# Loading the second expert behind the last row stores, and three expert matrices in sixteen pieces each

## The chip, the cores and the metric

The kernel runs on one core of a Trainium2 chip. The metric is the device time of one execution in microseconds (us). Before the change the median of three runs is 1216.72 us (1214.84 to 1219.3).

## What is computed

The input `x` is 2 sequences of 2048 tokens with 512 features (4096 tokens in all). One decoder layer in three stages, each fed by a layer norm and added back to `x`:

```
x = x + attn(layernorm(x))          # gated linear recurrence along the sequence
x = x + xattn(layernorm(x), ctx)    # 16 heads, 77 context tokens, causal mask
x = x + ffn(layernorm(x))           # mixture of 4 experts, the best 2 for each token

def ffn(x):                         # xf: the 4096 token rows
    gate_scores = xf @ gate_W + gate_b
    topk_scores, topk_idx = top_k(gate_scores, 2);  weights = softmax(topk_scores)
    h   = relu(layernorm(xf @ W1[e] + b1[e]) * g1[e] + be1[e])
    y_e = layernorm(h @ W2[e] + b2[e]) * g2[e] + be2[e]
    return xf + sum over the 2 chosen experts of weight * y_e
```

Each expert has two 512 x 512 matrices, W1 and W2. Everything is float32; the kernel splits each operand into a high and a low part and sums three products of the parts.

## The kernel before, in words

**Stages.** Stage A (the recurrence) and stage B (attention) each go over the tokens in 8 chunks of 512 (`NCH = 8`, `TPC = 4` tiles of 128 tokens in each). During stage A the eight expert matrices are split into high and low parts and stored in DRAM as `expert_parts` (`ws_d`), 2 MB for each matrix. Stage C is the mixture: 67 expert tiles (`NSLOT`), each with 128 rows of one expert. In stage B each token is given places in a slot table in DRAM, through indirect DMAs of GpSimd (`scatter`, L2513). The tokens of the first four chunks fill "early" tiles 0 to 28 (`EARLY = 29`), which are worked off from expert 0 to expert 3; the other 38 tiles follow, again from expert 0 to 3.

**One expert tile i** (`c_tile`): SyncE loads its 1 KB of slot entries (`load_slots`, L606); VectorE copies them to an index for the gather five tiles ahead (`gather_rows`, called in `c_tile` i - 5); GpSimd gathers the 128 rows (L2557, 256 KB); TensorE transposes them (`rows_in`, L1109), makes the first product with W1 (`first_product`, two tiles ahead, 12 matmuls at L1097), the transposes of the hidden rows (`hidden_in`, L1125) and the second product with W2 (`second_product`, 12 matmuls at L1097). So on TensorE the matmuls of `first_product(i + 2)` and `second_product(i)` stand together, 24 in one group. VectorE and ScalarE norm and scale. GpSimd adds the result rows to the output in DRAM with an indirect DMA that accumulates (`add_out`, L2576), and before it issues one it waits until the one before has landed: `need(pool, added[1 - u], 16 * (n + u))`. Behind that wait on GpSimd's own queue stand the next tile's reciprocal root (`rstd`, L2585), its gather and its slot scatter.

**Who waits for the weights.** The matrices have numbers s = 0 to 7: s = 2e is W1 of expert e and s = 2e + 1 its W2. SyncE raises `experts_ready` by one for each, in this order (`expert_in`). `first_product` waits for `experts_ready >= 2e + 1` (L1113) and `second_product` for `>= 2e + 2` (L1130). All DMAs that SyncE issues go to one queue, in program order, and a wait on SyncE holds everything written behind it.

**SyncE around the change.** It works off one written list (L613 to L669): matrix 0, the bias rows b1, slot pairs 0 to 2, matrix 4, row stores of chunk 6 (`store_xf` L547 to `xf_rows`, `store_base` L554 to the output), b2, matrix 1, more row stores, slot pairs 3 and 4, matrix 3, the last row stores, a wait for the base rows (`base_out`, L643), the g2 rows, and then matrices 2, 5, 6 and 7 between slot pairs 5 to 13. A slot pair is the loads of tiles 2n and 2n + 1, and a slot load waits for the one two before it. Behind the last matrix stand the four base stores of chunk 7, the waits for all row stores and for the slot table, and then the slot loads of tiles 28 to 66, of which tile 28's is first wanted in `c_tile` 23. ScalarE loads the be2 rows on its own queue (L1531) once the last `xf_rows` stores have landed.

Of the kernel before, what the change touches and what calls it, by code (L numbers as in the profile page):

```python
# [17 lines left out]
F32, F32R, I32 = mybir.dt.float32, mybir.dt.float32r, mybir.dt.int32  # L18
# [4 lines left out]
P = 128  # L23
B, S, D = 2, 2048, 512
T = B * S
KC = D // P
# [23 lines left out]
EARLY = 2 * EARLY_CH * TPC - (NE - 1)  # L50
# [16 lines left out]
def need(engine, semaphore, value):  # L67

    if isinstance(value, int) and value <= 0:
        return  # L70
    engine.wait_ge(semaphore, value)
# [9 lines left out]
def decoder_layer(nc, io, out, scratch_kind="Internal"):  # L81
    ctx = ExitStack()
    with ctx:
# [3 lines left out]
        def sem(name):  # L87
            return ctx.enter_context(nc.semaphore(name))
# [4 lines left out]
        def dram(name, shape, dt):  # L93
            return nc.dram_tensor(name, shape, dt, kind=scratch_kind).ap()
# [6 lines left out]
        ws_d = dram("expert_parts", [2 * NE, 2, KC, P, D], F32)  # L101
# [10 lines left out]
        def r_at(kb, n):  # L112
            return R[:, int(kb * KB_):int(kb * KB_) + n]
# [52 lines left out]
        weights = r_at(8, 4 * NE * KC * D).rearrange("p (w e a k f) -> p w e a k f", e=NE, w=2, a=2, k=KC)  # L166
# [122 lines left out]
        w_in = [sem(f"w_in{i}") for i in range(2 * NE)]  # L289
# [45 lines left out]
        def in_front(order, c):  # L335

            if isinstance(c, int):
                return sum(len(groups_of(order, i)) for i in range(-1, c))
            return in_front(order, 2) + (c - 2) * len(order)

        def index_in(order, c, name):
            return [g for g, _ in groups_of(order, c)].index(name)
# [5 lines left out]
        def mm_num(c, name):  # L348

            return in_front(MM_ORDER, c) + index_in(MM_ORDER, c, name)  # L350
# [4 lines left out]
        def last_in_bank(order, c, name):  # L355

            before_c = c - 1 if isinstance(c, int) else 1 if len(groups_of(order, 1)) == len(order) else 2
            own = groups_of(order, c)
            at = index_in(order, c, name)
            older = [] if isinstance(c, int) and c < 0 else groups_of(order, before_c)  # L360
            row = older + own[:at]
            same = [i for i, (_, bank) in enumerate(row) if bank == own[at][1]]
            return in_front(order, c) - len(older) + same[-1] + 1 if same else 0
# [7 lines left out]
        def slot3(c):  # L371

            return ring[:, (c + NCH) % 3] if isinstance(c, int) else ring[:, bass.ds((c + NCH) % 3, 1)].rearrange(
                "p r j f -> p (r j) f")
# [50 lines left out]
        def _(sp):  # L425
# [19 lines left out]
            for hl in range(HPG):  # L445
                rows = slice(hl * DH, (hl + 1) * DH)
# [103 lines left out]
            def store_base(c, j, rows=None):  # L550

                t = 4 * c + j
                need(sp, base_ready, t + 1)
                sp.dma_start(out_v[t] if isinstance(t, int) else out_v[bass.ds(t, 1)].rearrange("n p f -> p (n f)"),  # L554
                             base[:, j % 2] if rows is None else rows).then_inc(base_out[j % 2], 16)
# [31 lines left out]
            def load_expert(s):  # L587

                e, w = s // 2, s % 2
                sp.dma_start(weights[:, w, e].rearrange("p a k f -> p (a k) f").bitcast(F32),  # L590
                             ws_d[s].rearrange("a k p f -> p (a k) f")).then_inc(w_in[s], 16)

            def expert_in(s):
                sp.wait_ge(w_in[s], 16)
                sp.sem_inc(experts_ready, 1)

            def load_rows(dst, name, loaded):
                sp.dma_start(dst, io[name].rearrange("e f -> (e f)").partition_broadcast(P).rearrange(
                    "p (e f) -> p e f", e=NE)).then_inc(loaded, 16)

            def load_slots(n, u):

                i = 2 * n + u
                row = sp.value_load(plan_row[0:1, bass.ds(i, 1)], min_val=0, max_val=NE * REG - P)
                need(sp, slots_in[u], 16 * n)
                sp.dma_start(tile_slots[:, bass.ds(i, 1), :].rearrange("p i w -> p (i w)"),  # L606
                             slots_d[bass.ds(row, P), :]).then_inc(slots_in[u], 16)

            def load_slot_pairs(first, end):
                for n in range(first, end):  # L610
                    for u in range(2):
                        load_slots(n, u)
# [7 lines left out]
            sp.wait_ge(plan_ready, 1)  # L620
            load_slot_pairs(0, 3)
            expert_in(0)
            sp.wait_ge(s_done, 2 * KC * NCH)
            load_expert(4)
# [8 lines left out]
            for j in range(2):  # L633
                store_base(last - 1, j, slot3(last - 1)[:, j, :])
            load_slot_pairs(3, 5)
            load_expert(3)
            for j in range(2, TPC):
                store_base(last - 1, j, slot3(last - 1)[:, j, :])
            sp.wait_ge(mm_done, mm_num(NCH, "o3") + 1)
            for j in range(TPC):  # L640
                store_xf(last, j)
            for i in range(2):
                sp.wait_ge(base_out[i], 16 * 2 * last)  # L643
            load_rows(g2_rows, "L0_ffn_g2", g2_in)
            expert_in(1)
            load_slot_pairs(5, 7)
            load_expert(2)
            load_slot_pairs(7, 9)
            for s in range(2, 5):
                expert_in(s)  # L650
            for s in range(5, 2 * NE):
                load_expert(s)
                load_slot_pairs(2 * s - 1, min(2 * s + 1, EARLY // 2))
                expert_in(s)
            for j in range(TPC):
                store_base(last, j, slot3(last)[:, j, :])
# [1981 lines left out]
```

## Time and profile before

| | us |
|---|---|
| median of 3 runs (range) | 1216.72 (1214.84 to 1219.3) |
| the profiled execution's own time | 1209.59 |
| its span | 1207.8 |
| TensorE (PE) busy | 1159.6 (96%) |
| VectorE (DVE) busy | 924.9 (77%) |
| ScalarE (ACT) busy | 731.5 (61%) |
| GpSimd (POOL) busy | 457.2 (38%) |

How to read it: the span is the stretch of the profiled execution from its first to its last instruction, and every time in rows counts in us from its start. PE is busy nearly all the time, so what can be saved are its few idle stretches; an idle stretch of another engine costs nothing by itself. PEclk is the clock that TensorE was granted, 1.00 being 2.4 GHz and 0.50 being 1.2 GHz. "To landing" is the time from the issue of a DMA to its arrival.

### The profile page before, as it was taken

How to read it: one execution, taken by the hardware profiler on the slowest of the kernel's cores; microseconds unless marked ns; L12 is line 12 of the kernel's file. 1: busy time of each engine (PE TensorE's matmuls, PEld its weight loads, DVE VectorE, ACT ScalarE, POOL GpSimd, SP SyncE). 2: the span in 40 equal slices, each digit the busy share in tenths (PEclk: the TensorE clock that was granted, in tenths of full speed). 3: DMA queues.
4: the chain of work that ended last, by engine and by line, in shares of the span. 5: the costliest groups of instructions: out<-in, count | busy, mean ns of one | idle time of the engine just before them, and what ended most of it. 6: DMA issues, size and time to landing. Idle time of an engine off the chain costs nothing.

```text
span 1207.8 us, 24523 instructions
## 1 busy us (share of the span) xinstructions
PE 1159.6 (96%) x6041; PEld 978.9 (81%) x6042; DVE 924.9 (77%) x2196; ACT 731.5 (61%) x2114; POOL 457.2 (38%) x410
## 2 busy tenths in 40 slices
PE   6999999999989999999999998989999999999993
PEld 5788888888878888888888877867888888888882
DVE  6888888887766677877868777678777777777774
ACT  5323333233486757767677662567777777777773
POOL 4040000000052314535445164357655555555543
PEclk9999999999999999999999998899999999999998
DMA  8754544444520302133021358885554444444433
GB/s 271 230 160 160 188 176 146 174 156 165 199 84 1 105 10 97 44 107 104 10 97 44 131 131 227 270 221 122 81 88 81 85 79 86 80 85 80 85 64 42
DMA packets 83237, 143.90 MB, mean 119 GB/s; under 512 B 20460, under 2 KB 24752, under 8 KB 82309
## 3 DMA queue, kind: packets, MB, share of 16 engines
q1 hardware_dynamic: 63872, 101.60, 25.8%
q0 software_dynamic: 18464, 39.14, 17.1%
q10 hardware_dynamic: 837, 2.41, 0.6%
q8 instruction: 28, 0.46, 0.2%
q14 instruction: 36, 0.29, 0.1%
HBM read 78.83 MB, written 67.83 MB: 121 GB/s over the span
## 4 chain that ended last, share of the span: by engine, by line
PE 83%; DMA 5%; DVE 4%; issue 3%; ACT 3%; POOL 2%; POOLq 0%; DVEq 0%; SPq 0%; ACTq 0%
PE banks L1097 27%; PE banks L681 21%; PE banks L746 7%; PE banks L891 6%; PE banks L879 5%; DMA out<-rows,scatter_rows 4%; PE banks L848 3%; PE banks L865 3%; PE banks L1109 2%; PE banks L907 2%; PE banks L1125 2%; ACT rows L1310 2%; PE banks L719 1%; PE banks L800 1%; PE banks L765 1%
## 5 line engine op out<-in xcount | busy, mean ns | idle before, releaser
L1097 PE MATMUL banks<-operands 128*128 x1608 | 388.6, 396 | 10.5 <-DVE operands L1570 5.2
L1097 PEld LDWEIGHTS banks<-operands 128*128 128x128 f32 x1608 | 298.1, 189 | 73.6 <-issue 7.4
L681 PE MATMUL banks<-operands 128*128 128x512 f32 (+2 forms) x1224 | 292.6, 394 | 3.5 <-DVE operands L1570 3.5
L681 PEld LDWEIGHTS banks<-operands 128*128 128x128 f32 (+1 forms) x1224 | 225.6, 192 | 47.8 <-DVE operands L1570 3.7
L1570 DVE TENSOR_TENSOR operands<-banks,operands 128x512 fp32r<-128x512 f32 (+3 forms) x328 | 217.7, 682 | 42.5 <-ACT operands L1189 38.8
L1189 ACT ACTIVATE operands<-banks 128x512 fp32r<-128x512 f32 (+3 forms) x328 | 191.7, 608 | 96.7 <-PE banks L879 45.0
L1310 ACT ACTIVATE rows<-banks,score_shift 128x77 f32<-128x77 f32 x512 | 162.7, 374 | 28.0 <-DVE score_shift L1792 27.2
L1189 ACT ACTIVATE operands<-rows 128x512 fp32r<-128x512 f32 (+3 forms) x79 | 55.3, 709 | 163.8 <-DVE rows L1641 138.1
L1495 ACT ACTIVATE banks<-banks,param_cols 128x128 f32<-128x128 f32 x268 | 99.2, 430 | 82.5 <-PE banks L1125 82.5
L2576 POOL DMA_INDIRECT out<-rows,scatter_rows x67 | 106.6, 1591 | 104.2 <-DVE rows L2315 65.1
L1310 ACT ACTIVATION_READ_ACCUMULATOR rows<-banks,score_shift 128x1 f32 x512 | 129.1, 256 | 0.0
L2500 POOL TENSOR_TENSOR rows<-rows,score_rec 128x1232 f32<-128x1232 f32 x32 | 72.1, 2253 | 147.3 <-DVE score_rec L1800 147.3
L2262 DVE BATCH_NORM_STATS2 moe_stats<-banks 128x6 f32<-128x512 f32 x134 | 93.2, 695 | 43.9 <-PE banks L1097 42.5
L891 PE MATMUL banks<-operands 128*128 128x512 f32 x384 | 97.7, 406 | 0.0
L746 PE MATMUL banks<-operands 128*128 128x512 f32 x384 | 91.6, 394 | 0.1
L2585 POOL TENSOR_TENSOR moe_rstd<-moe_var_eps,minus_half 128x2 f32<-128x2 f32 (+1 forms) x70 | 52.4, 748 | 83.8 <-DVE moe_var_eps L2275 83.8
L746 PEld LDWEIGHTS banks<-operands 128*128 128x128 f32 x384 | 70.9, 188 | 15.7 <-DVE operands L1570 1.3
L891 PEld LDWEIGHTS banks<-operands 128*128 128x128 f32 x384 | 72.0, 194 | 14.2
L2557 POOL DMA_INDIRECT rows<-xf_rows,gather_rows x67 | 69.3, 1034 | 30.8 <-issue 24.9
L879 PE MATMUL banks<-operands 103*128 103x512 f32 (+1 forms) x288 | 75.6, 403 | 2.0 <-DVE operands L1783 1.4
L2460 POOL TENSOR_TENSOR ln_rstd<-ln_var_eps,minus_half 128x4 f32 (+1 forms) x8 | 10.1, 1262 | 170.8 <-DVE ln_var_eps L1665 170.8
L2513 POOL DMA_INDIRECT slot_table<-slot_payload,slot_rows x64 | 65.1, 1018 | 19.8 <-issue 13.7
(178 smaller groups left out, 1707.0 us busy)
## 6 DMA issues: line engine op xcount, KB each, us to landing
expert_parts<-operands SPq DMA_DIRECT2D x32, 512.0 KB, 3.0
operands<-expert_parts SPq DMA_DIRECT2D x8, 2048.0 KB, 11.1
rows<-in_x SPq DMA_DIRECT2D x8, 1024.0 KB, 5.4
rows<-in_L_ffn_W SPq DMA_DIRECT2D x32, 256.0 KB, 3.5
x_rows<-rows SPq DMA_DIRECT2D x8, 1024.0 KB, 4.3
rows<-x_rows SPq DMA_DIRECT2D x8, 1024.0 KB, 5.7
xf_rows<-rows SPq DMA_DIRECT2D x32, 256.0 KB, 2.7
out<-rows SPq DMA_DIRECT2D x32, 256.0 KB, 2.5
```

Of the source, the lines that this page charges most:

```text
L681: last = nc.tensor.matmul(dst, stationary(a, k), moving(b, k), start=(t == 0 and k == 0), stop=(t == len(terms) - 1 and k == n_k - 1))
L746: last = nc.tensor.matmul(g_bank[m % 2], wg[:, a, k, m * P:(m + 1) * P], hTr[:, a2, k, :], start=(k == 0 and t == 0), stop=(k == KC - 1 an ...
L879: last = nc.tensor.matmul(mb(c, f"v{m}"), vblk[0:n, a, m, u, :], pT[0:n, a2, u, :], start=(t == 0 and u == 0), stop=(t == len(TERMS) - 1 a ...
L891: last = nc.tensor.matmul(mb(at, f"o{j}"), out_part(c, a, m)[:, j * P:(j + 1) * P], wo[:, a2, m, :], start=(m == 0 and t == 0), stop=(m == ...
L1097: last = nc.tensor.matmul(dst, stationary[:, a, k, :], weights[:, w, bass.ds(e, 1), a2, k, :].rearrange("p e f -> p (e f)"), start=False, ...
L1189: return nc.scalar.activation(dst, src, ACT.Copy, scale=scale)
L1310: nc.scalar.activation(pb[m % 2][:, j, keys], s_banks[:, j, keys], ACT.Exp, bias=nmax[:, m % 2, at], scale=-1.0, accum_out=ssum[:, m % 2, ...
L1495: nc.scalar.activation(ch_bank[:, at], ch_bank[:, at], ACT.Relu, scale=pcol[:, bass.ds(e * KC + (ROW_G1 + k), 1)], bias=pcol[:, bass.ds(e ...
L1570: return V.tensor_tensor(dst, src, hi.bitcast(F32), ALU.subtract)
L2262: V.bn_stats(c_st[:, which, :], src).then_inc(stat, 1)
L2500: G.tensor_tensor(p3, p3, srec[:, m % 2, :].unsqueeze(2).to_broadcast([P, TPC * HPG, SK]), ALU.mult).then_inc(p_ready, 1)
L2576: G.indirect_dma_start(out, bass.IndirectOffsetOnAxis(six[u][:, 0:1], 0), y2[u], None, compute_op=ALU.add).then_inc(added[u], 16)
```

## The change

Four things are changed, all in SyncE's list.

- Matrix 3 (W2 of expert 1) is no longer loaded between slot pair 4 and the last base stores of chunk 6, but behind the g2 rows and matrix 2.
- `expert_in(1)` moves ahead of the wait for the last projection and the row stores of chunk 7.
- Slot pairs 5 to 8 come in one row behind matrices 2 and 3, where matrix 2 stood between pairs 6 and 7.
- Matrices 5, 6 and 7 are not one DMA of 2 MB each, but sixteen of 64 partitions x 2 KB (128 KB) each. Before each piece but the first SyncE waits until the piece before has landed, so one is in flight at a time. A slot pair follows each half of a matrix, and `expert_in(s)` waits for all sixteen.

```diff
+            PIECES = 4 * KC
+
+            def load_expert_parts(s, parts):
+                e, w = s // 2, s % 2
+                for n in parts:
+                    a, k, rows = n // (2 * KC), n // 2 % KC, slice(n % 2 * (P // 2), (n % 2 + 1) * (P // 2))
+                    need(sp, w_in[s], 16 * n)
+                    sp.dma_start(weights[rows, w, e, a, k, :].bitcast(F32), ws_d[s, a, k, rows]).then_inc(w_in[s], 16)
+
             def expert_in(s):
-                sp.wait_ge(w_in[s], 16)
+                sp.wait_ge(w_in[s], 16 if s < 5 else 16 * PIECES)
                 sp.sem_inc(experts_ready, 1)
...
             load_slot_pairs(3, 5)
-            load_expert(3)
             for j in range(2, TPC):
                 store_base(last - 1, j, slot3(last - 1)[:, j, :])
+            expert_in(1)
             sp.wait_ge(mm_done, mm_num(NCH, "o3") + 1)
             for j in range(TPC):
                 store_xf(last, j)
             for i in range(2):
                 sp.wait_ge(base_out[i], 16 * 2 * last)
             load_rows(g2_rows, "L0_ffn_g2", g2_in)
-            expert_in(1)
-            load_slot_pairs(5, 7)
             load_expert(2)
-            load_slot_pairs(7, 9)
+            load_expert(3)
+            load_slot_pairs(5, 9)
             for s in range(2, 5):
                 expert_in(s)
             for s in range(5, 2 * NE):
-                load_expert(s)
-                load_slot_pairs(2 * s - 1, min(2 * s + 1, EARLY // 2))
+                for half_n in range(2):
+                    pair = 2 * s - 1 + half_n
+                    load_expert_parts(s, range(PIECES // 2 * half_n, PIECES // 2 * (half_n + 1)))
+                    load_slot_pairs(pair, min(pair + 1, EARLY // 2))
                 expert_in(s)
```

## Rows read from the trace of the kernel before

**Rows 1.** The page, busy time of each engine (share of the span), instructions.
```profile
PE 1159.6 (96%) x6041; PEld 978.9 (81%) x6042; DVE 924.9 (77%) x2196; ACT 731.5 (61%) x2114; POOL 457.2 (38%) x410
```

**Rows 2.** TensorE's timeline, 736 to 880: start, us, line, operation, [idle before <-releaser].
```profile
753.53 0.66 PE L1109 MATMUL banks<-ident,rows 128*128 128x128 f32 x4 [2.39 <-DMA rows<-xf_rows,gather_rows]
...
759.27 7.40 PE L1097 MATMUL banks<-operands 128*128 x24
...
768.53 5.78 PE L1097 MATMUL banks<-operands 128*128 x24
...
788.18 1.20 PE L1097 MATMUL banks<-operands 128*128 x4 [1.98 <-DVE operands L1570]
...
803.51 1.79 PE L1097 MATMUL banks<-operands 128*128 x4 [2.29 <-DVE operands L1570]
...
819.04 1.19 PE L1097 MATMUL banks<-operands 128*128 x4 [0.92 <-DVE operands L1570]
...
827.50 5.71 PE L1097 MATMUL banks<-operands 128*128 x24
...
833.84 5.73 PE L1097 MATMUL banks<-operands 128*128 x24
```

**Rows 3.** The chain that ended last, 690 to 1210: start, us, what.
```profile
784.25 4.92 DMA out<-rows,scatter_rows
790.02 8.94 DMA out<-rows,scatter_rows
...
903.95 5.46 PE banks L1097 x24
```

**Rows 4.** GpSimd's timeline, same columns as TensorE's.
```profile
743.30 0.98 POOL L2557 DMA_INDIRECT rows<-xf_rows,gather_rows  x1 [0.30 <-issue]
```

**Rows 5.** Waits, 700 to 1210: us in total, times, longest.
```profile
POOL out L2576 <- DMA out<-rows,scatter_rows: 21.5, 11, 4.3
```

**Rows 6.** Windows of 4 us: PE, PEld, DVE, ACT, POOL, PEclk, DMA share, GB/s.
```profile
756.00:760.00 4.00, 4.00 (x19) 3.90 (x20) 1.05 (x4) 0.21 (x1) 2.00 (x2) 0.51 1.03 412
760.00:764.00 4.00, 4.00 (x13) 3.14 (x12) 1.98 (x11) 0.56 (x1) 0.00 (x0) 0.64 1.00 319
```

**Rows 7.** SyncE's timeline, 650 to 1210: first start, us to the last issue's end.
```profile
742.44 0.43 SPq L590 DMA_DIRECT2D operands<-expert_parts  x1
...
744.08 3.85 SPq L547 DMA_DIRECT2D xf_rows<-rows  x4
756.23 0.34 SPq L598 DMA_DIRECT2D rows<-in_L_ffn_g  x1
...
775.65 0.40 SPq L590 DMA_DIRECT2D operands<-expert_parts  x1
...
802.41 0.40 SPq L590 DMA_DIRECT2D operands<-expert_parts  x1
...
815.19 1.90 SPq L554 DMA_DIRECT2D out<-rows  x4
872.55 63.17 SPq L606 DMA_DIRECT2D rows<-slot_table  x39
```

**Rows 8.** SyncE's waits, 650 to 1000: us in total, times, longest.
```profile
SPq L643 <- DMA out<-rows: 8.2, 1, 8.2
```

**Rows 9.** DMA issues, 742 to 744.3: count, KB each, median us to landing.
```profile
operands<-expert_parts SPq DMA_DIRECT2D x1, 2048.0 KB, 12.4
```

**Rows 10.** DMA issues, 802 to 803, and then 815 to 818.
```profile
operands<-expert_parts SPq DMA_DIRECT2D x1, 2048.0 KB, 12.7
...
out<-rows SPq DMA_DIRECT2D x4, 256.0 KB, 2.6
```

**Rows 11.** The page, DMA issues of the whole span: two loads of 1 MB and 256 KB.
```profile
rows<-in_x SPq DMA_DIRECT2D x8, 1024.0 KB, 5.4
...
rows<-in_L_xattn_Wq SPq DMA_DIRECT2D x4, 256.0 KB, 2.7
```

**Rows 12.** Line L466, eight single loads of 256 KB into SBUF.
```profile
DMA to landing us min/median/max: 2.5/2.7/4.3
```

## Prediction

> **What bounds the kernel now.** I read the page first: TensorE is busy for 1159.6 of 1207.8 us [rows 1], so only its idle stretches (and its slow ones) can be won. Next I read TensorE's timeline where the expert matrices are loaded. The reader is to see there that a tile in the undisturbed stretch takes 833.84 - 827.50 = 6.34 us, while from 768.53 to 827.50 eight tiles take 58.97 us instead of 8 x 6.36 = 50.9 (6.36 is the mean of twelve tiles, (903.95 - 827.50) / 12 = 6.37) [rows 2, 3]. That is 8.1 us lost, with idle stretches of 1.98, 2.29 and 0.92 us in the middle of the second product. The trace names VectorE for them; the chain of waits and GpSimd's waits say who is behind it: the accumulating DMA takes 8.94 us instead of 4.92 when it meets a matrix of 2 MB (one row stands for three alike), and GpSimd waits 21.5 us for it in all [rows 3, 5]. The next tile's reciprocal root stands behind that wait, and the hidden rows behind the root. Ahead of this a gather issued at 743.30 lands only when TensorE has waited 2.39 us for it, at 753.5: matrix 3 was issued just before it, at 742.44 [rows 2, 4, 7]. Last I read SyncE's timeline, for when each matrix is issued, and the DMA issues for how long each size takes.
>
> **Part 1: matrix 3 moves behind the row stores.** The gather of 743.30 then meets only six row stores of 256 KB, and at less than half its present 10 us it is there before TensorE asks at 751.1: -2.4 us. The stretch is also the one after which the granted clock fell to 0.51 and 0.64 [rows 6], and the 24 matmuls of 759.27 took 7.40 instead of 5.7 us [rows 2]. If less idle time keeps the clock up, about 1.7 us more is won here; I leave that out of the sum, since other idle time stays in the stretch, and keep it for the lower end.
>
> SyncE gains too. It waited 8.2 us for base stores that were queued with matrix 3 [rows 8], so the g2 rows go out at about 748.0 (744.08 + 3.85) instead of 756.23, and matrices 2 and 3 by 748.9 [rows 7]. The queue then holds 1 + 2 + 2 MB, and the be2 rows (1 MB) come on ScalarE's queue. Matrix 3 took 12.4 us with 1.5 MB of stores about it, so 3.5 MB in 12.4 us [rows 9]; 5 MB take 18 us by this, 6 MB 21. I take 19: all in at 767.5. Eight slot loads stand behind; the first two are issued at once, the third waits for the first, which lands behind the matrices. The other six cost 1.62 us each (39 of them in 63.17 us [rows 7]), less a little: SyncE reaches the pieces at T0 = 776 us, 770 to 781. It was 775.65 when matrix 5 went out before [rows 7], so SyncE arrives at the same time with matrix 3 behind it. `expert_in(2)` comes at T0 as well. It is wanted by `first_product(5)` in `c_tile` 3, which began two tiles behind 768.53 (`c_tile` 1 [rows 2]), at 781.3, and after part 1 begins at about 779: hidden, with 3 us to spare. It costs what T0 is later than that, up to 2 us. `expert_in(1)` moves past nothing that anybody waits for: matrix 1 is long in, and TensorE did not wait for it. The larger risk of the part is that the next gathers now meet 5 MB. The program issues a gather two tiles, 12.7 us, ahead of its use, and that of 743.30 took 10 us in like company [rows 2, 4], so nothing.
>
> **Part 2: what the pieces remove.** Between 776 and 815 three loads of 2 MB filled the queue. In pieces of 128 KB, one in flight, an accumulating DMA meets at most one piece on each engine. I take 4.9 to 5.5 us for it, against the 6.36 of a tile: GpSimd no longer falls behind and the 8.1 us go. The bounds of this term are 0 (pieces disturb as much as whole matrices) and -8.1. Together G = 2.4 + 8.1 = 10.5 us.
>
> **Part 3: what the pieces add.** SyncE now pays one full flight for each of 48 pieces where it paid three such as 12.7 us [rows 10]. The trace shows no 128 KB load, so it is bounded. Single loads of 256 KB landed in 2.5 us at least, 2.7 in the median, 4.3 at worst [rows 12]. From 1 MB at 5.4 to 256 KB at 2.7 is 2.7 us for 768 KB, so half of 256 KB saves 0.45 us [rows 11]: 2.05 to 2.25 us. Beside the mixture's gathers and accumulating DMAs four stores of 256 KB landed in 2.6 at 815 us [rows 10], which is no more than the loads' median, so for that company I add only 0.1 to the upper of the two. To this comes 0.08 us from landing to the next issue (the last matrix: 802.41 + 12.7 = 815.11, next issue 815.19 [rows 7, 10]). One step is then t = 2.4 us. Its bounds are 2.1, and 2.9 if the pieces meet the other DMAs at every step. A slot pair takes 2 x 1.62 + 0.4 us of SyncE beside one flight, so each of the five pairs adds 3.6 - t = 1.2.
>
> All of matrix 7 is in at A = T0 + 48 t + 5 (3.6 - t) = 776 + 115.2 + 6 = 897 us, where it was 815.1.
>
> **When is it wanted?** From the reference's inputs the two choices of the first 2048 tokens are 697, 1052, 1151 and 1196 for experts 0 to 3, in whole tiles 5, 8, 8 and 9. So expert 1 starts at tile 5, expert 2 at 13, expert 3 at 21. Tile 9's group began at 827.50 and tile 21's at 903.95 [rows 2, 3]; the second product is its later half, so in the old time W2 of expert 3 (matrix 7) is wanted at 906.8. Matrix 6 is wanted in `c_tile` 19, at 891; matrix 5 in `c_tile` 13, at 856. They arrive at T0 + 32 t + 5 = 858 and 817: both hidden. The slots of tile 26, wanted in `c_tile` 21, go out at T0 + 40 t + 6 = 878: hidden until t is over 2.7.
>
> With a gain G ahead of tile 21 everything is wanted G earlier, and matrix 7 holds TensorE if it is later. The two do not add up; the change in the end is the larger of -G and A - 906.8. That is the larger of -10.5 and -9.8: **about 1 us of stall, net -9.8**. For one more microsecond or so of stall and clock I take -8.5. Slot loads of tiles 28 and on come behind A, four stores (1.90 us) and their landing (2.6), at about 903, where they began at 872.55 [rows 7, 10]. Tile 28's is wanted in `c_tile` 23, old time 916.6, new 906.6, and needs some 3 us more: hidden by about 1 us, and if matrix 7 is late, that moves with it.
>
> **A rule of the skill.** The Trainium skill, "DMA: Bandwidth & Descriptors", section "Rules for kernel authors", speaks against the change: merge small transfers, at least 1 MiB for full bandwidth. The trace agrees as to bandwidth (2 MB in 12.4 to 12.7 us [rows 9, 10] against 16 x 2.4 = 38). Its section "Anatomy of one DMA" gives about 2.0 us and bytes / 436 GB/s for the GpSimd path; that would be 2.3 us for a piece, an estimate by that page, and with the 0.08 A = 896, the same case.
>
> **Rivals.**
> 1. *The weights' own latency takes the gain.* At t = 2.6, A = 906.7: the end does not move at all, and from there each 0.1 us in t costs 4.3 us. In t = 2.48 to 2.7 the result is within 6 us of before, -6 to +5. For it: 256 KB loads were 2.7 in the median. Against it: half the bytes.
> 2. *Slower.* The one mechanism is the same wait, of `second_product(21)` for `experts_ready >= 8`, at t over 2.73 (or 2.6 with T0 six us late). At t = 2.9, A = 776 + 139.2 + 3.5 = 918.7: +12 us, and after such an idle stretch the clock may fall as in [rows 6], +2: **+14**. For it: 256 KB took 4.3 us at worst [rows 12]. Against it: the median of eight is 2.7.
> 3. *The pieces disturb as much as the matrices did*, and the change doesn't do what it says. Then G = 2.4 and the end moves by -2.4, no more, as matrix 7 is wanted at 904. Against it: at most a few packets lie ahead of an accumulating DMA.
> 4. *All hidden, and the clock stays up*: G = 12.2 and t of 2.3 or less, -12.
>
> **How the numbers follow.** Forecast (with rival 4): 50%. Rival 1: 18%. Rival 3: 8%. Rival 2: 24%, as one number multiplied by 48 decides, and T0 shifts it too. The sum is made against the profiled execution: span 1207.8, own time 1209.6, so it would come out at 1201.1. The median of the runs shown is 1216.7, 7.1 above that execution, and the same change on it gives **1208.2 us**. The low end is rival 4's -12: 1204.5. The high end reaches into rival 2, +12: 1228.5. The likeliest case alone is 1204.5 to 1211. 0.5% is 6.1 us, about what a measurement of this kernel can tell from no change: faster 0.50, same 0.25, slower 0.25.
>
> **What would show it.** Right: the waits for L2576 by GpSimd shrink from 21.5 us to under 8; no accumulating DMA of 8.9 us; the gather of tile 3 in under 6 us and no 2.39 on L1109; SyncE's pieces from about 776, 2.4 us apart; TensorE's only wait for experts is at tile 21 and is under 3 us. Wrong: pieces over 2.6 us apart, with a hole in TensorE before the second product of tile 21, of the size A - 896; a hole before tile 5's first product (T0 late); or idle time on L1097 as before with no long transfer on SyncE's queue.

## The result, and the profile after

The changed kernel takes 1254.89 us in the median of 4 runs (1251.24 to 1256.15), beside 1217.97 us for the kernel before on the same chip (the three runs shown ahead and one more). The ratio is 1.0302 with a 95% interval of 1.0271 to 1.0333: 37 us slower, where I had forecast 8.5 faster. The measured time also lies above the range (1204.5 to 1228.5).

The page of the profile after. Its span is 46.0 us longer than before, at the same work of TensorE (1163.3 us where [rows 1] have 1159.6). Five loads of 2 MB are left of the eight.

```profile
span 1253.8 us, 24568 instructions
PE 1163.3 (93%) x6041; PEld 979.5 (78%) x6042; DVE 925.7 (74%) x2196; ACT 731.0 (58%) x2114; POOL 455.3 (36%) x410
...
operands<-expert_parts SPq DMA_DIRECT2D x5, 2048.0 KB, 9.2
```

The waits after, 700 to 1250 us (us in total, times, longest). TensorE waits for SyncE three times, 45.6 us in all, which is about the size of the difference. (Added up: its busy time grew by 3.7 us and its idle time by 42.3, of which the 45.6 are one part and 3.3 us less of other idle time the other.) VectorE's waits for slot entries (22.3 us) fall in the same stretch; none of them shows in TensorE's waits. GpSimd's wait for its accumulating DMAs, the thing the pieces were to cure, is down from 21.5 us [rows 5] to 15.0.

```profile
PE banks L1108 <- SPq L605: 45.6, 3, 27.1
...
DVE gather_rows L2292 <- DMA rows<-slot_table: 22.3, 3, 11.2
...
POOL out L2587 <- DMA out<-rows,scatter_rows: 15.0, 8, 3.6
```

TensorE's timeline after, 740 to 990 us, with the columns of [rows 2]. The three long idle stretches stand at `c_tile` 3, 19 and 21: they are tile 5's first product (matrix 2), tile 21's first product (matrix 6) and tile 21's second product (matrix 7). Between 796.98 and 829.28 a tile takes 6.46 us, so the idle stretches of 2 us at tiles 3 to 7 in [rows 2] are gone, as is the wait of 2.39 us for the gather of tile 3.

```profile
774.60 5.84 PE L1108 MATMUL banks<-operands 128*128 x24
...
788.06 8.29 PE L1108 MATMUL banks<-operands 128*128 x24 [6.74 <-SPq L605]
...
796.98 5.71 PE L1108 MATMUL banks<-operands 128*128 x24
...
829.28 3.01 PE L1108 MATMUL banks<-operands 128*128 x12
...
906.38 7.23 PE L1108 MATMUL banks<-operands 128*128 x24 [11.73 <-SPq L605]
...
920.61 2.98 PE L1108 MATMUL banks<-operands 128*128 x12
950.69 4.51 PE L1108 MATMUL banks<-operands 128*128 x12 [27.11 <-SPq L605]
```

SyncE's timeline after, with the columns of [rows 7]: first start, and the time to the end of the last issue. The g2 rows go out at 755.45, the slot loads behind 5 MB take 27.26 us, the pieces begin at 788.11 and the last has landed at 950.59, when the base stores go out. Eight issues in 31.52 us are seven steps of (31.52 - 0.47) / 7 = 4.44 us.

```profile
755.45 0.58 SPq L608 DMA_DIRECT2D rows<-in_L_ffn_g  x1
756.08 3.43 SPq L590 DMA_DIRECT2D operands<-expert_parts  x2
760.57 27.26 SPq L616 DMA_DIRECT2D rows<-slot_table  x8
788.11 24.53 SPq L601 DMA_DIRECT2D operands<-expert_parts  x8
813.90 2.25 SPq L616 DMA_DIRECT2D rows<-slot_table  x2
816.17 31.52 SPq L601 DMA_DIRECT2D operands<-expert_parts  x8
...
851.31 28.76 SPq L601 DMA_DIRECT2D operands<-expert_parts  x8
...
882.33 21.42 SPq L601 DMA_DIRECT2D operands<-expert_parts  x8
...
906.10 20.87 SPq L601 DMA_DIRECT2D operands<-expert_parts  x8
...
929.23 19.23 SPq L601 DMA_DIRECT2D operands<-expert_parts  x8
950.59 1.82 SPq L554 DMA_DIRECT2D out<-rows  x4
```

The six groups have steps of 3.44, 4.44, 4.04, 2.99, 2.91 and 2.68 us, 3.42 in the mean. They are shorter while TensorE stands still and the mixture issues few DMAs of its own; the slot scatters, too, had ended at 871 us. So the first three groups, 3.97 us in the mean, show the company of the running mixture. The windows say so too (columns as in [rows 6]): a DMA share of 0.70 while the mixture runs, 0.31 while it stands, and 0.17 from 940 to 948 us, where none of the other engines is busy and the pieces are alone.

```profile
816.00:882.00 66.00, 65.73 (x329) 54.17 (x328) 53.23 (x150) 49.83 (x104) 43.10 (x41) 1.00 0.70 114
...
929.00:950.00 21.00, 0.00 (x0) 0.00 (x0) 3.77 (x10) 2.38 (x4) 2.62 (x2) 0.50 0.31 75
...
940.00:948.00 8.00, 0.00 (x0) 0.00 (x0) 0.00 (x0) 0.00 (x0) 0.00 (x0) 0.50 0.17 49
```

The chain of waits in that last stretch has these single flights, from issue to landing:

```profile
940.63 2.39 DMA operands<-expert_parts
943.04 2.53 DMA operands<-expert_parts
945.59 2.39 DMA operands<-expert_parts
```

A step of 2.4 us, as forecast, is thus what a 128 KB piece takes beside nothing (940.63 to 943.04), and not what it takes beside the running mixture.

### The profile page after: what moved, and what is told of

It reads as the page before. It is cut to its first block, busy times and chain, and to the rows that moved or that the text cites. A ratio compares the mean times of both kernels' runs of the same rounds, so it can differ in the third digit from the quotient of the medians.

```text
span 1253.8 us, 24568 instructions
## 1 busy us (share of the span) xinstructions
PE 1163.3 (93%) x6041; PEld 979.5 (78%) x6042; DVE 925.7 (74%) x2196; ACT 731.0 (58%) x2114; POOL 455.3 (36%) x410
## 4 chain that ended last, share of the span: by engine, by line
PE 62%; DMA 11%; issue 9%; DVE 7%; SPq 5%; ACT 3%; POOL 1%; DVEq 0%; POOLq 0%; ACTq 0%
PE banks L1108 19%; PE banks L692 15%; DMA operands<-expert_parts 7%; PE banks L757 6%; PE banks L902 5%; PE banks L890 5%; PE banks L859 3%; PE banks L876 3%; DMA rows<-slot_table 2%; ACT rows L1321 2%; PE banks L1136 2%; PE banks L1120 1%; DVE operands L1581 1%; PE banks L918 1%; SPq L616 1%
## 5 line engine op out<-in xcount | busy, mean ns | idle before, releaser
L1108 PE MATMUL banks<-operands 128*128 x1608 | 395.1, 401 | 53.0 <-SPq L605 45.6
L859 PE MATMUL banks<-operands 128*128 128x308 f32 (+1 forms) x384 | 71.9, 312 | 0.0
```

Of the source, the lines that this page charges most:

```text
L859: last = nc.tensor.matmul(s_banks[:, j, :], qT[:, a, m, j * P:(j + 1) * P], keys, start=(t == 0), stop=(t == len(TERMS) - 1 and j > 0))
L1108: last = nc.tensor.matmul(dst, stationary[:, a, k, :], weights[:, w, bass.ds(e, 1), a2, k, :].rearrange("p e f -> p (e f)"), start=False, ...
```

## The experiments

Theory F: 48 flights in a row make matrix 7 late. Its rivals: the small transfers use the engines badly in any order (B), or the new order with 5 MB on the queue is what costs (Q). "Before" is the kernel before, run on the same chip beside the experiment. Experiments 1 to 4 share one chip (before: 1212.95 us), 5 to 8 another (1212.59), and 9 to 11 a third (1217.82). One and the same kernel varies by some 8 to 12 us from execution to execution there, so each ratio is to be read with its 95% interval, and times or starts read from two single traces can differ by several us for no other reason.

**All sixteen in flight.**

```diff
                 for n in parts:
...
-                    need(sp, w_in[s], 16 * n)
```

> The changed kernel without the wait between the pieces: still sixteen DMAs of 128 KB for each of matrices 5 to 7, all in flight. Theory F (one flight at a time: the 48 landings in a row make matrix 7 late): the last matrix is in by about 840 us instead of 950, the two stalls at tile 21 (11.7 and 27.1 us) are gone, the one at tile 5 (6.7 us) stays, and accumulating DMAs of 8 to 9 us come back: 1215 to 1224 us. Rival B (128 KB transfers of 2 KB rows use the DMA engines badly in any order): matrix 7 still comes after 900 us, 1240 us or more.

Measured: 1204.59 us, before 1212.95, ratio 0.9923 (0.9899 to 0.9947). Rival B falls: the same 48 transfers, not held back, make the kernel faster than before. So it takes the cut alone, and not one piece in flight at a time, to win what the pieces can win. The last matrix is in when the base stores go out, at 833.02; in SyncE's timeline the issues themselves pace the pieces, at 0.7 us:

```profile
823.64 5.58 SPq L600 DMA_DIRECT2D operands<-expert_parts  x8
833.02 1.87 SPq L554 DMA_DIRECT2D out<-rows  x4
```

I had expected 1215 to 1224, because accumulating DMAs of 8 to 9 us would come back. In the chain of waits the longest took 7.40 us, and TensorE's idle stretches behind them were 1.3 us in all, where before had 5.2 [rows 2]. The stall at tile 5 was 2.3 us and not 6.7.

**Pieces in the old order.** The kernel before with `load_expert_parts` and its loop put in, and nothing moved:

```diff
-                load_expert(s)
-                load_slot_pairs(2 * s - 1, min(2 * s + 1, EARLY // 2))
+                for half_n in range(2):
+                    pair = 2 * s - 1 + half_n
+                    load_expert_parts(s, range(PIECES // 2 * half_n, PIECES // 2 * (half_n + 1)))
+                    load_slot_pairs(pair, min(pair + 1, EARLY // 2))
```

(`expert_in` waits for all sixteen here as well.)

> The kernel before with matrices 5 to 7 in one-in-flight pieces, and nothing else changed. Theory F: SyncE begins the pieces at about 776 and needs the 162 us that they took in the changed kernel, so matrix 7 is in at about 938, wanted at 907: 31 us late, 1244 to 1252 us, with no stall at tile 5. Rival Q (the new order with 5 MB in one row on the queue is what costs): under 1225 us.

Measured: 1251.24 us, ratio 1.0277 (1.0223 to 1.0332). SyncE's timeline has the first piece at 785.31 and the base stores at 948.11; there is no stall at tile 5. The pieces, one in flight, give the loss without the new order.

```profile
785.31 28.27 SPq L601 DMA_DIRECT2D operands<-expert_parts  x8
...
948.11 1.83 SPq L554 DMA_DIRECT2D out<-rows  x4
```

**The new order with whole matrices.** The changed kernel with the old loop over matrices 5 to 7:

```diff
-                sp.wait_ge(w_in[s], 16 if s < 5 else 16 * PIECES)
+                sp.wait_ge(w_in[s], 16)
...
-                for half_n in range(2):
-                    pair = 2 * s - 1 + half_n
-                    load_expert_parts(s, range(PIECES // 2 * half_n, PIECES // 2 * (half_n + 1)))
-                    load_slot_pairs(pair, min(pair + 1, EARLY // 2))
+                load_expert(s)
+                load_slot_pairs(2 * s - 1, min(2 * s + 1, EARLY // 2))
```

> The changed kernel's order, with matrices 5 to 7 as single DMAs of 2 MB. Theory F: the stall of some 7 us at tile 5 stays, and the slow clock behind it (2 to 3 us), against 1 to 2 us won from the gather of tile 3; matrix 7 is in by about 830: 1220 to 1228 us. Rival Q: 1240 us or more. The prediction's part 1 would have 1214 to 1216.

Measured: 1214.08 us, before 1212.95, ratio 0.9991 (0.9955 to 1.0027): no difference. (The median lies where part 1 would have it, but the kernel before was at 1212.95 here, so that agreement is luck.) Rival Q falls. I had put theory F at 1220 to 1228 for it, and that was too much: TensorE's wait at tile 5 was 2.57 us here. With whole matrices the slow accumulating DMAs are there as before (9.46 and 9.44 us at worst), and so are TensorE's idle stretches behind them (2.63 and 1.91 us).

```profile
784.12 5.73 PE L1106 MATMUL banks<-operands 128*128 x24 [2.57 <-SPq L605]
```

**Telling TensorE of matrix 2 before the slot loads.**

```diff
             load_expert(3)
+            expert_in(2)
             load_slot_pairs(5, 9)
-            for s in range(2, 5):
+            for s in range(3, 5):
```

> The changed kernel with the step that tells TensorE of matrix 2 (expert_in(2)) ahead of slot pairs 5 to 8. The stall at tile 5 should go. If the arrival of matrix 7 alone sets the end (the larger of gain and lateness, theory F), nothing is won by it: 1251 to 1257 us, and the 6.7 us appear again as longer stalls at tile 21. If stalls add up (rival), 1243 to 1249.

Measured: 1247.64 us, ratio 1.0266 (1.0225 to 1.0307), which lies below what I had given theory F (1251 to 1257) and within what I had given its rival, that stalls add up (1243 to 1249); its interval overlaps that of the changed kernel. The time alone thus speaks for the rival, if for anything. The trace speaks for theory F: the stall at tile 5 is gone, yet TensorE still waits 40.7 us for SyncE, nearly all of it at tile 21 (12.95 and 27.41 us, where the changed kernel has 11.73 and 27.11). What I had not expected is that the pieces began at 782.27, six us earlier than in the changed kernel; the last had landed at 942.12, 8.5 us earlier, and the span is 6.9 us shorter. So the end moved with matrix 7's arrival. About half of the earlier start was there before the edit has any effect: SyncE was at the g2 rows at 752.66, not at 755.45.

```profile
782.27 28.99 SPq L601 DMA_DIRECT2D operands<-expert_parts  x8
...
942.12 1.82 SPq L554 DMA_DIRECT2D out<-rows  x4
```

and its waits, 700 to 1210 us:

```profile
PE banks L1109 <- SPq L605: 40.7, 3, 27.4
```

**Two in flight.**

```diff
-                    need(sp, w_in[s], 16 * n)
-                    sp.dma_start(weights[rows, w, e, a, k, :].bitcast(F32), ws_d[s, a, k, rows]).then_inc(w_in[s], 16)
+                    need(sp, w_in[s - 5 * (n % 2)], 16 * (n // 2 + n % 2))
+                    sp.dma_start(weights[rows, w, e, a, k, :].bitcast(F32),
+                                 ws_d[s, a, k, rows]).then_inc(w_in[s - 5 * (n % 2)], 16)
...
-                sp.wait_ge(w_in[s], 16 if s < 5 else 16 * PIECES)
+                sp.wait_ge(w_in[s], 16 if s < 5 else 8 * PIECES)
+                if s >= 5:
+                    sp.wait_ge(w_in[s - 5], 16 + 8 * PIECES)
```

> The changed kernel with two pieces of 128 KB in flight in place of one (two counters, each piece waits for the one two before it). Theory F: 24 waits of some 4 us in a row take the place of 48 of 3.3, matrix 7 is in at about 885 to 895, before it is wanted: 1203 to 1212 us, and the stalls at tile 21 are gone. Rival B (the pieces share what the mixture's DMAs leave of the engines, so two take twice as long as one): no change, 1245 us or more.

Measured: 1206.03 us, before 1212.59, ratio 0.9937 (0.9911 to 0.9962). A flight takes 4.2 us in the median, and since two run at once the step is (13.59 - 0.47) / 7 = 1.87 us in the group shown, the second of six. Matrix 7 is in at 884.36, and TensorE waits for SyncE only at tile 5 (5.3 us). Flights that lengthened in proportion to their number would have left the step at 3.4 or more.

```profile
797.79 13.59 SPq L601 DMA_DIRECT2D operands<-expert_parts  x8
...
884.36 2.48 SPq L554 DMA_DIRECT2D out<-rows  x4
```

and for line L601:

```profile
DMA to landing us min/median/max: 2.5/4.2/4.9
```

**Eight pieces of 256 KB.**

```diff
-            PIECES = 4 * KC
+            PIECES = 2 * KC
...
-                    a, k, rows = n // (2 * KC), n // 2 % KC, slice(n % 2 * (P // 2), (n % 2 + 1) * (P // 2))
+                    a, k = n // KC, n % KC
...
-                    sp.dma_start(weights[rows, w, e, a, k, :].bitcast(F32), ws_d[s, a, k, rows]).then_inc(w_in[s], 16)
+                    sp.dma_start(weights[:, w, e, a, k, :].bitcast(F32), ws_d[s, a, k]).then_inc(w_in[s], 16)
```

> The changed kernel with eight pieces of 256 KB (128 partitions) per matrix, one in flight. If a flight is mostly a fixed price plus the wait for the mixture's packets (theory F), it is 3.7 to 4.2 us where 128 KB is 3.3, 24 of them 90 to 100 us: matrix 7 in at about 890, 1203 to 1212 us. If a flight grows with its bytes (6.6 us), nothing is gained: 1245 us or more.

Measured: 1204.7 us, ratio 0.9941 (0.9921 to 0.9961). The pieces begin at 780.08 and matrix 7 is in at 874.47. A step takes 3.9 us in the first three groups, no more than the 3.97 of the pieces of half the size. Line L601's 24 flights:

```profile
DMA to landing us min/median/max: 2.6/3.9/5.3
```

**Four pieces of 512 KB**, cut in the same way (two of the four row blocks of one part in each).

> The changed kernel with four pieces of 512 KB per matrix, one in flight. Theory F: 12 flights of 4.5 to 5.5 us, matrix 7 in by about 860; accumulating DMAs are disturbed somewhat more than by smaller pieces: 1204 to 1214 us. The rival of the prediction that any bytes disturb alike would have 1214 or more, with three accumulating DMAs over 8 us.

Measured: 1212.85 us, before 1212.59, ratio 0.9977 (0.9946 to 1.0008), which shows no gain; its profiled execution (1204.4 us) was one of its faster ones. The flights took 5.0 us in the median, matrix 7 was in at 843.68, and the longest accumulating DMA in the chain of waits took 7.24 us, where I had the rival at over 8.

```profile
DMA to landing us min/median/max: 3.9/5.0/6.6
```

**A plain copy for the accumulating DMA.** The mixture's rows are written over the output and not added to it, so this kernel leaves out a part of the computation and its output is not that of the layer.

```diff
-                G.indirect_dma_start(out, bass.IndirectOffsetOnAxis(six[u][:, 0:1], 0), y2[u], None,
-                                     compute_op=ALU.add).then_inc(added[u], 16)
+                G.indirect_dma_start(out, bass.IndirectOffsetOnAxis(six[u][:, 0:1], 0), y2[u], None).then_inc(added[u], 16)
```

> The changed kernel, but the mixture's result rows are written to the output and not added to it: the indirect DMA of each tile is a plain copy of 256 KB, which reads nothing back. It measures what a 128 KB flight costs beside less traffic. If the accumulating DMA is what stretches the flights from 2.4 us (seen while TensorE stood still) to 3.4 to 4.4 beside the running mixture, the first 24 pieces take under 3.3 us each, matrix 7 comes 20 us earlier or more, and the time is 1215 to 1235 us. If it is the gathers and the slot DMAs, the pieces keep their pace: 1248 to 1256.

Measured: 1234.88 us in two executions, ratio 1.0177 (1.0126 to 1.0229). The first three groups of pieces have steps of 3.03, 3.27 and 3.52 us, 3.27 in the mean, where the changed kernel has 3.97. That is 0.7 of the 1.6 us by which a step beside the mixture is longer than one beside nothing (2.4). It is the price of adding in place of writing, since the rows are still written here; gathers, slot DMAs and plain row writes are left for the rest, and I have not parted them. Of the 21 us by which matrix 7 came earlier (929.16 for 950.59), 4.8 are an earlier first piece (783.30). In the window of 816 to 848 us the DMA share falls from 0.71 (first line, the changed kernel) to 0.50 (second line, this one):

```profile
816.00:848.00 32.00, 31.73 (x155) 25.54 (x154) 27.65 (x82) 24.33 (x50) 20.53 (x21) 1.00 0.71 112
...
816.00:848.00 32.00, 32.00 (x163) 26.86 (x162) 27.66 (x83) 24.70 (x52) 18.83 (x21) 1.00 0.50 127
```

**Pieces of 256 KB, and matrix 2 told early** (the edits of the fourth and the sixth experiment together).

> Eight pieces of 256 KB per matrix, one in flight, and expert_in(2) ahead of slot pairs 5 to 8: meant to be the better of both. With the larger-of-two rule matrix 7 (in at about 872, wanted at some 897) no longer sets the end, so here the stall at tile 5 and the slow clock behind it (3 to 4 us in e6) come off the end: 1199 to 1203 us. If stalls at tile 5 are taken back later by something else, no better than e6, 1204 to 1206.

Measured: 1204.29 us, before 1217.82, ratio 0.989 (0.9863 to 0.9916). The ratio is the lowest of all, 1.1% faster than before; no wait for SyncE is left among TensorE's, and matrix 7 is in at 877.31. But the median lies above the 1199 to 1203 that I expected, in the range that I had given the rival (no better than the sixth experiment, 1204 to 1206), and that experiment has 1204.7. What puts the two ratios apart is before: 1217.82 us on this chip, 1212.59 on that of the sixth experiment. Beside the other two experiments on its own chip it is 4 us faster, with intervals that overlap. So whether the step that tells TensorE of matrix 2 early wins anything is not shown.

**Matrix 3 behind slot pairs 5 and 6**, pieces of 256 KB.

```diff
             load_expert(2)
-            load_expert(3)
-            load_slot_pairs(5, 9)
-            for s in range(2, 5):
+            load_slot_pairs(5, 7)
+            load_expert(3)
+            expert_in(2)
+            load_slot_pairs(7, 9)
+            for s in range(3, 5):
```

> Eight pieces of 256 KB, and matrix 3 behind slot pairs 5 and 6, so that 3 MB and not 5 MB stand on the queue when the first slot load is issued. Theory K (the issue of a slot load is held for 8 to 9 us because the queue is full of the rows of g2 and two matrices): no slot load's issue over 2 us, the pieces begin 6 to 10 us earlier than in e6 (780), at 770 to 774, no stall at tile 5: 1199 to 1204 us. If the slot loads only wait for landing, the pieces begin at about 780 as in e6.

Measured: 1208.6 us, ratio 0.9931 (0.9904 to 0.9957), where I had expected 1199 to 1204. Half of theory K held. With 5 MB ahead of it one slot load's issue was held for 7.88 us (first fence, the changed kernel); with 3 MB the longest of ten took 1.88 (second fence; ns, min/median/max). But the pieces did not begin earlier: at 789.13, with TensorE's timeline some 5 us later as a whole, where that of the sixth experiment had 780.08 (this trace is of the slowest of its six executions, that one of the fastest of nine). The stall at tile 5 is gone, as expected; the one idle stretch that still names SyncE's count (2.21 us) stands at tile 1's first product, where the changed kernel has 2.17 us under ScalarE's name. The time not spent in issuing was spent in waiting for the slot loads to land: 16.4 us in all, where the sixth experiment has 9.3. And matrix 3, issued whole at 775.62 into the running mixture, brings back what part 2 describes: the accumulating DMA of 778.23 takes 8.60 us (third fence), and TensorE has 4.0 us of idle stretches behind VectorE.

```profile
L616 SPq DMA_DIRECT2D rows<-slot_table x2: 382/4130/7877, 760.6 to 769.6; - x2
```

```profile
L616 SPq DMA_DIRECT2D rows<-slot_table x10: 3/346/1878, 749.8 to 789.0; - x10
```

```profile
778.23 8.60 DMA out<-rows,scatter_rows
```

**Pieces of 256 KB in the old order.**

> The kernel before with matrices 5 to 7 in eight pieces of 256 KB each, one in flight; order as before. Shows what the pieces alone are worth: the stalls of 8.1 us at tiles 3 to 7 go, the wait for the gather of tile 3 stays: ratio 0.993 to 0.996, 1204 to 1208 us. If the new order brings the gain, no better than before.

Measured: 1208.05 us, ratio 0.9927 (0.9904 to 0.9951). The time lies at the upper end of what I expected and the ratio at the lower. From `c_tile` 1 to 9 TensorE takes 52.9 us, where before took 59.0 [rows 2]: 6.0 of the 8.1 us are back, and no idle stretch behind VectorE is left. The pieces are worth 0.7% by themselves where they are in on time (matrix 7 at 885.02).

## Why the prediction was wrong

- **The place and the rule were right.** Tile 21 was the one at which matrices 6 and 7 were wanted, `c_tile` 19 and 21, and the end moves with A, the arrival of matrix 7. By the forecast's rule, A - 906.8 (the time of [rows 3] at which it was wanted before) is 43.8 us for the changed kernel, 41.3 for the pieces in the old order, 35.3 and 22.4 for the fourth and eighth experiments. Their spans grew by 46.0, 43.3, 39.1 and 23.1. The part over the rule is 0.7 to 3.8 us, no more than executions of one kernel differ; the slow restart is in it (the 12 matmuls behind the long stall took 4.51 us where 12 take 3.0). Matrix 6 was to be hidden (858 for 891) and was late as well: TensorE stood 11.73 us for it, up to 906.38. By the same rule that adds nothing, as matrix 7 came later still.
- **The step that failed is the size of t** in part 3, one flight with its issue, and in it the 0.1 us for the company of the mixture's DMAs. I had 2.4 us, bounds 2.1 and 2.9; it was 3.42 in the mean, 4.44 in the worst group. Over 42 steps within groups that is 143.5 us for 101, 43 us of the 54 by which A was later (950.6 for 897). The base was nearly right: 2.05 to 2.25 us for a quiet flight, where quiet ones took 2.39 to 2.53. The addition for the mixture's DMAs was not: I took 0.1 us from four stores (not loads) at 815 us [rows 10], one moment, where it is 1.6 us in the first three groups, and the eighth experiment shows the adding of the accumulating DMAs to hold 0.7 of it. The upper bound was wrong for the same reason; the one row that pointed beyond it (4.3 us at worst, [rows 12]) I gave to the rival as an accident.
- **T0 was 12 us late**, 788.1 for 776. SyncE came to the g2 rows at 755.45 and not 748: it reached slot pairs 3 and 4 at 732.07, 5.6 us later than before (726.48 in its trace), and these took 20.05 us for 15.92. From the g2 rows to the first piece it was 32.7 us, where I had 28; I had the first two slot loads go out at once, and the issue of the first was held for 7.88 us. Nothing shows that the new order makes T0 late: the two versions in the old order have their first piece at 785.31 and 786.59, and the profiled execution of before was early with 775.65. Rival 2 had this case, at t of 2.9: A = 918.7. With the measured t and T0 its formula gives 788 + 48 x 3.42 + 5 x 0.2 = 953, and the measured value is 950.6. (By that formula A is 905.8 at t = 2.6, where rival 1 says 906.7, and 12 us about 1216.7 give a range of 1204.7 to 1228.7; neither changes the argument.)
- **Matrix 2's stall at tile 5** was 6.74 us where I had up to 2. It cost the end nothing, since matrix 7 came later still. In the versions in which matrix 7 is on time it is 2.0 to 5.3 us; whether taking it away wins that is not shown (ninth experiment).
- **Part 1's gain** (the gather of tile 3) was there in the traces: from the first product of tile 0 to `c_tile` 1 the changed kernel takes 1.2 us less than before's 27.8, not 2.4, and the nine other versions in the new order take 1.9 to 3.9 less, while the two in the old order take 2.2 and 3.1 more. It did not reach the end by itself: the order alone has a ratio of 0.9991, as its stall at tile 5 (2.57 us) and the idle stretches behind whole matrices come after. The granted clock fell in that stretch all the same (0.65 in 760 to 764).
- **Part 2's gain** was right in mechanism: no idle stretch of TensorE behind an accumulating DMA is left at `c_tile` 3 to 8, and it is 0.7% in the old order with pieces that are on time. Rival 3 fell. The sign that I had named for it was a bad one, though: GpSimd's waits for accumulating DMAs shrank to 15.0 us here, not under 8, and in the versions that are faster than before they are 27.3 to 33.0 us in all, about what before has (21.5, and 7.8 more that the trace puts down to VectorE). What goes with the gain is the longest of them: 4.3 us before, 5.4 with whole matrices in the new order, and 3.3 to 3.6 in the faster versions.
- **Not settled:** which of the gathers, slot DMAs and row writes make up the other 0.9 us of a step.

## What to carry to other kernels

A chain of dependent transfers costs flights x number, and the flight has to be taken from the company that it will have, not from single quiet ones: here 2.4 us alone and 3.4 to 4.4 beside gathers, slot scatters and accumulating DMAs. Cutting a load to spare its neighbours pays as long as the last piece lands before it is wanted; two in flight, or twice the size, gave the same relief in about six tenths of the time (100 and 94 us for 162), and all in flight gave it in 52. When a number is to be multiplied by 48, its bounds matter more than its value.

## What the runs showed of the hardware

A flight grows little with its size beside the mixture: a step (landing and issue) of 128 KB took 3.97 us in the first three groups and one of 256 KB 3.9, and the flights of 256 KB and 512 KB took 3.9 and 5.0 us in the median. A small DMA's issue on SyncE can be held when much is queued ahead of it: with 5 MB just issued it was held for 7.88, 8.98 and 9.51 us (the changed kernel, the sixth and the third experiment), at most 1.88 behind 3 MB, and 0.38 where SyncE had first waited for matrix 2 to land (the fourth). That what is queued is the reason is inferred from these five. An accumulating DMA of 256 KB took 8.2 to 9.5 us beside a matrix of 2 MB and 5.3 to 7.4 beside pieces, one or all in flight. The Trainium skill, "DMA: Bandwidth & Descriptors", "Rules for kernel authors", asks for at least 1 MiB in one DMA. As to bandwidth the runs agree (2 MB in 12.4 to 12.7 us [rows 9, 10], 256 KB in 3.9), but the kernel with 256 KB pieces was faster than with 2 MB ones (0.9927), although its last matrix was in only at 885 us and not at 815.
